# Attention halves of sixteen steps: last scores, value products in groups of four and output copies run in the next half

## The reference, cut

```python
x = x + attn(layernorm(x))                   # 16 heads of 8, 128 tokens against themselves
x = x + cross_attn(layernorm(x), ctx, mask)  # 16 heads of 8, 128 tokens against 77
x = x + moe(layernorm(x))                    # gate on L2-normed projection, top 2 of 8 experts

def attention(q_in, kv_in):                  # the same shape for both
    q, k, v = heads(q_in @ Wq.T), heads(kv_in @ Wk.T), heads(kv_in @ Wv.T)
    scores = einsum("bhqd,bhkd->bhqk", q, k) * scale      # cross: where mask == 0, -1e9
    return einsum("bhqk,bhkd->bhqd", softmax(scores), v) @ Wo.T + bias

def moe(x):                                  # h [8, 64, 128, 512]
    comb = sum(one_hot(top_i, 8) * softmax(top_v)[..., None], -2)
    h = gelu(einsum("bsd,edf->ebsf", x, W1) + b1)
    return einsum("ebsd,bse->bsd", einsum("ebsf,efd->ebsd", h, W2) + b2, comb)
```

## Time and profile before

| what | value |
|---|---|
| three runs | 1179.84, 1180.71, 1183.54 us |
| median | 1180.71 us |
| the profiled execution | 1185.62 us, its span 1183.9 us |
| TensorE busy over the span | 996.1 us, 84% |
| ScalarE | 799.0 us, 67% |
| VectorE | 749.3 us, 63% |
| GpSimd | 593.3 us, 50% |
| mean granted TensorE clock | 0.941 of full speed |
| DMA | 144.16 MB, mean 122 GB/s |

### The profile page before, as it was taken

One profiled execution on the slowest core, in us unless ns is written; L12 is line 12 of the kernel. 1 busy time (PEld: TensorE's weight loads), 2 busy tenths in 40 slices (PEclk: granted clock), 3 DMA queues, 4 the chain that ended last, 5 costly groups with the idle time before them and its releaser, 6 DMA issues. The chain is left out here.

```text
span 1183.9 us, 31785 instructions
## 1 busy us (share of the span) xinstructions
PE 996.1 (84%) x11621; PEld 767.5 (65%) x11621; DVE 749.3 (63%) x2074; ACT 799.0 (67%) x1649; POOL 593.3 (50%) x821
## 2 busy tenths in 40 slices
PE   2567889999999999999999999847529999999940
PEld 1345667777777777777777777635418888888830
DVE  2554746666667666676666674423258888888836
ACT  2144557777777777777777777635419999999930
POOL 4313423365655664664654643544534666666650
PEclk9997999999999999999999999978759999999975
DMA  3337684455455555545545642230452444232319
GB/s 92 83 75 157 141 187 102 120 142 146 128 151 134 134 136 140 142 126 140 151 112 147 147 110 73 57 81 31 136 161 76 125 129 113 79 83 75 84 56 372
DMA packets 120387, 144.16 MB, mean 122 GB/s; under 512 B 34189, under 2 KB 98528, under 8 KB 115432
## 3 DMA queue, kind: packets, MB, share of 16 engines
q1 hardware_dynamic: 108888, 120.33, 40.0%
q0 software_dynamic: 9168, 17.21, 4.8%
q10 hardware_dynamic: 2176, 4.59, 1.0%
HBM read 88.38 MB, written 55.36 MB: 121 GB/s over the span
## 5 line engine op out<-in xcount | busy, mean ns | idle before, releaser
L615 ACT ACTIVATE probs<-sc_a 77x512 f32<-77x512 f32 (+1 forms) x512 | 301.0, 592 | 148.5 <-PE sc_a L1008 93.2
L757 DVE TENSOR_REDUCE negm_m<-sc_m 128x4 f32<-128x512 f32 x256 | 169.5, 683 | 82.5 <-PE sc_m L987 81.4
L1305 POOL DMA_INDIRECT y_d<-yo,row x156 | 160.7, 1030 | 115.0 <-DVE yo L1419 73.6
L757 DVE TENSOR_REDUCE negm_cm<-sc_m 128x4 f32<-128x308 f32 x256 | 119.1, 471 | 144.5 <-PE sc_m L992 143.0
L477 POOL DMA_INDIRECT xs_d<-xrow,slot_i x128 | 131.9, 1031 | 121.3 <-PE sc_a L1008 80.0
L1022 PE MATMUL pv<-probs,big 128*32 128x128 f32 x4096 | 165.7, 280 | 0.6
L987 PE MATMUL sc_m<-ks,qs 96*128 96x128 bf16 x1024 | 105.3, 230 | 37.5 <-DMA ks<-stk_k 13.4
L1022 PEld LDWEIGHTS pv<-probs,big 128*32 128x32 f32 x4096 | 96.3, 109 | 56.2 <-ACT probs L615 28.6
L1400 DVE TENSOR_TENSOR gl<-g,gh 128x512 fp32r<-128x512 f32 x156 | 107.4, 689 | 35.1 <-ACT g L1349 34.6
L987 PEld LDWEIGHTS sc_m<-ks,qs 96*128 96x128 bf16 x1024 | 71.6, 102 | 82.6 <-issue 55.8
L1003 PE MATMUL sc_a<-cqs,cks 102*77 102x128 bf16 x1024 | 102.0, 223 | 4.9 <-DMA cqs<-cmscr 4.8
(11 more groups left out here) (202 smaller groups left out, 2333.7 us busy)
## 6 DMA issues: line engine op xcount, KB each, us to landing
xg<-xs_d SPq DMA_DIRECT2D x39, 260.0 KB
stk_q<-parts_q SPq DMA_DIRECT2D x16, 384.0 KB, 2.9
stk_k<-parts_k SPq DMA_DIRECT2D x16, 384.0 KB, 2.7
qs<-stk_q SPq DMA_DIRECT2D x16, 384.0 KB, 5.9
ks<-stk_k SPq DMA_DIRECT2D x32, 192.0 KB
stk_cq<-parts_cq SPq DMA_DIRECT2D x16, 384.0 KB, 2.9
cqs<-stk_cq SPq DMA_DIRECT2D x16, 384.0 KB
xin<-x_dram SPq DMA_DIRECT2D x16, 256.0 KB
```

Source lines behind the costliest of these rows:

```text
L615: nc.scalar.activation(probs[e % 4][0:rows], sc_a[e % 2][0:rows], ACT.Exp, scale=scale)\
L757: nc.vector.tensor_reduce(out=negm[n][:, s, HG * g + 4 * half:HG * g + 4 * half + 4], in_=sc_m[u % 2][:, 0:4 * cols].rearrange("p (j k) -> ...
L1305: nc.gpsimd.indirect_dma_start(out=y12_d, in_=yo[par][:, c, :], in_offset=None, bounds_check=2 * B * S - 1, oob_is_err=False, out_offset=b ...
```

## The change

A half has 16 steps (`STEPS = UNITS`). What stood in steps 16 to 18 of a half runs inside the first steps of the next: the last unit's `shifted` in step 0, the last four units of `values` in step 2 and the second output copy on ScalarE in step 3. `values` runs in groups of four units, in steps 2, 6, 10 and 14, where before it ran in groups of two. There are seven `probs` tiles (`NP`) in place of four, used in rotation across halves (`probs_of`). The waits for whole halves between two halves are gone: each unit waits for the unit two before it, across the boundary too, and the waits for a half's stacks and folded maxima stand in step 1 (`own_ready`, `cross_ready`).

The tables of side work are written anew on all engines. The output transposes are in steps 2 and 5 of X and 2 and 4 of Y (before: 0 and 1), each output's product in step 9 of X and 8 of Y (before: 5). The transposes of the normalised rows for the cross queries, the cross query product and its splitting into parts move from the end of Y into steps 1 to 6 of the following X, with `dump` and `stack` of "cq". In Y `mark` goes from step 13 to 15, and `weigh` and `route` go into the next X. On SyncE's queue the fold of "m" stands ahead of the stack of "k". GpSimd's body has its pieces in another order to match. No product, exponential, maximum or DMA is added or left out.

The diff, cut to its core:

```diff
-STEPS = UNITS + LEAD + 2
+STEPS = UNITS
...
+NP = 7
...
+        def probs_of(n, b, u):
+
+            half = 2 * b if n == "s" else 2 * b + 5
+            return probs[(UNITS * half + u) % NP]
...
-                        for n, dst in (("cq", cqs), ("ck", cks)):
-                            wait_block(sp, st_f["c"], t - 3)
-                            stack(n, t - 1, dst[1 - par])
+                        wait_block(sp, st_f["c"], t - 3)
+                        stack("ck", t - 1, cks[1 - par])
+                        dump("cq", t - 1)
+                        stack("cq", t - 1, cqs[1 - par])
...
                         fold("m", t + 1, qs[1 - par])
...
+                    if on_(t + 2):
+                        stack("k", t + 2, ks[par])
...
+                    if on_(t - 1):
+                        third("cq", t - 1)
...
+                def exponential(attn, e, before):
...
+                    n, b, rows, scale = attn
+                    act.wait_ge(st_f[n].sem, st_f[n].val(b, e + 1))
+                    if e >= NP:
+                        act.wait_ge(pv_ok[n].sem, pv_ok[n].val(b, e - NP + 1))
+                    elif before:
+                        act.wait_ge(pv_ok[before[0]].sem, pv_ok[before[0]].val(before[1], UNITS - NP + e + 1))
...
+                        if u == 0 and before:
+                            exponential(before, UNITS - 1, None)
+                        if u > 0 and attn:
+                            exponential(attn, u - 1, before)
+                        if u == 3 and before:
+                            out_T(before[0], before[1], 1)
+                        if u == 12 and attn:
+                            out_T(attn[0], attn[1], 0)
                         between(u)
-                    if on_(b):
-                        out_T(n, b, 1)
...
+                        if u == 2 and on_(t - 1):
+                            evac(xnT["2"][:], "x2T", t - 1, 1)
+                        if u == 4 and on_(t - 1):
+                            first("cq", t - 1, bq_c)
+                        if u == 6 and on_(t - 1):
+                            second("cq", t - 1)
...
+                        if u == 8 and on_(t - 3):
+                            evac(onT["c"][:], "onT_c", t - 3, 1)
...
+                        if u == 12 and on_(t):
                             evac(cT[:], "cT", t, 1, TC)
...
+                        if u == 7 and on_(t):
                             evac(onT["s"][:], "onT_s", t, 1)
...
+                        if 12 <= u < 12 + NS and on_(t):
+                            normalise("2", t, x2, u - 12)
+                        if u == 15 and on_(t - 3):
                             act.wait_ge(dv_ok.sem, dv_ok.val(t - 3))
                             nc.scalar.activation(ev[:], dv[:], ACT.Exp).then_inc(ev_ok.sem, 1)
...
+                        if u == 0 and on_(t - 4):
+                            weigh(t - 4)
+                        if u == 1 and on_(t - 4):
+                            route(t - 4)
+                        if u == 3 and on_(t - 3):
+                            divide("c", t - 3, 0)
+                        if u == 4 and on_(t - 1):
+                            wait_block(dve, part3["q"], t + 1)
+                            remainder("cq", t - 1, bq_c)
                         if u == 6 and on_(t - 3):
+                            divide("c", t - 3, 1)
+                        if u == 10 and on_(t - 3):
                             wait_block(dve, x3_st, t - 4)
                             add_residual("c", t - 3, x2res[1 - par], x3)
-                        if u == 7 and on_(t - 3):
...
-                        if u == 12 and on_(t):
+                        if u == 15 and on_(t):
                             wait_block(dve, part3["ck"], t - 1)
                             remainder("ck", t, bk_c)
...
+                        if u == 3 and on_(t):
+                            divide("s", t, 0)
+                        if u == 5 and on_(t):
+                            divide("s", t, 1)
...
                             choose(t - 3)
-                        if u == 13 and on_(t - 3):
+                        if u == 14 and on_(t - 3):
+                            point(t - 3)
+                        if u == 15 and on_(t - 3):
                             mark(t - 3)
...
-                        if u == 18 and on_(t):
-                            wait_block(dve, part3["q"], t + 2)
-                            remainder("cq", t, bq_c)
...
                         pe.wait_ge(max_ok[n].sem, max_ok[n].val(b, u - 1))
+                    else:
+                        wait_block(pe, max_ok[last[0]], last[1], UNITS - 1 + u)
...
+                    else:
+                        wait_block(pe, exp_ok[last[0]], last[1], UNITS - 1 + u)
...
 
                     for u in range(STEPS):
-                        if maxi and u < UNITS:
+                        if maxi:
                             scores(maxi[0], maxi[1], u, *maxi[2:])
-                        if attn:
-                            n, b, qst, kst, va, cols, bias, last = attn
-                            if LEAD <= u < UNITS + LEAD:
-                                shifted(n, b, u - LEAD, qst, kst, cols, bias)
-                            if u >= LEAD + 2 and u % 2 == 0:
-                                values(n, b, u - LEAD - 3, va, last)
-                                values(n, b, u - LEAD - 2, va, last)
+                        if u == 0 and before:
+                            shifted(before[0], before[1], UNITS - 1, *before[2:])
+                        if u == 1 and attn:
+                            ready()
+                        if u > 0 and attn:
+                            shifted(attn[0], attn[1], u - 1, *attn[2:])
+                        if u == 2 and before:
+                            for v in range(UNITS - 4, UNITS):
+                                values(before[0], before[1], v, *before[2:])
+                        if u >= 6 and u % 4 == 2 and attn:
+                            for v in range(u - 6, u - 2):
+                                values(attn[0], attn[1], v, *attn[2:])
                         between(u)
...
                     def in_x(u):
-                        if u < NO and on_(t - 3):
-                            outputs_T("c", t - 3, u)
-                        if u == 3 and on_(t - 3):
+                        if u == 1 and on_(t - 1):
+                            pe.wait_ge(ln_ok["2"].sem, ln_ok["2"].val(t - 1))
+                            transposes("x2T", t - 1, 1, [xn["2"][:, s, :] for s in range(NS)], 128)
+                        if u == 2 and on_(t - 3):
+                            outputs_T("c", t - 3, 0)
+                        if u == 3 and on_(t - 1):
+                            pe.wait_ge(drained["x2T"].sem, drained["x2T"].val(t - 1))
+                            product("cq", t - 1, cw_q[:], xnT["2"][:], T)
+                        if u == 5 and on_(t - 3):
+                            outputs_T("c", t - 3, 1)
+                        if u == 5 and on_(t - 1):
+                            by_token("cv", t - 1, 0, cT, cw_v[:], D, SC)
+                        if u == 7 and on_(t - 3):
                             divided_T("c", t - 3)
-                        if u == 4 and on_(t - 1):
...
                             project("c", t - 3, cw_o)
-                        if u == 6 and on_(t - 2):
-                            maxima_T("cm", t - 2)
...
-                        if u == 11 and on_(t):
+                        if u == 13 and on_(t):
                             pe.wait_ge(drained["cT"].sem, drained["cT"].val(t))
...
-                        if u < NO and on_(t):
-                            outputs_T("s", t, u)
-                        if u == 3 and on_(t):
+                        if u == 2 and on_(t):
+                            outputs_T("s", t, 0)
+                        if u == 4 and on_(t):
+                            outputs_T("s", t, 1)
+                        if u == 4 and on_(t + 1):
...
+                        if u == 8 and on_(t):
                             project("s", t, w_ff)
...
-                        if u == 16 and on_(t):
-                            pe.wait_ge(drained["x2T"].sem, drained["x2T"].val(t))
-                            product("cq", t, cw_q[:], xnT["2"][:], T)
...
+                    beside(own(t), cross(t - 3), maxi, own_ready, in_x)
...
+                    beside(cross(t - 2), own(t), maxi, cross_ready, in_y)
```

219 lines of the change are left out of this document (93 added, 126 removed).

## The result

The changed kernel took 1235.95 us (median of four, 1233.89 to 1237.25) beside 1182.12 for the kernel before; the ratio is 1.0455, interval 1.043 to 1.0481. Run again unedited as a control, on a chip on which the kernel before took 1191.89 us, it took 1240.98: 1.0401 (1.037 to 1.0432). The forecast was slower, 1206, with a range to 1230. The direction held, the size did not: the cost is about twice the forecast, and above the range. The control came out a little under the first ratio; the two intervals meet at their edges.

The account below looks back on a forecast made before the run. TensorE's own queue was taken as the bound. Per iteration 5.3 - 1.6 - 2.1 = +1.6 us, +19 over twelve, +6 for filling and draining: 1185.62 + 25 = 1210.6, less 4.9 for the median, 1206 us; range 1188 to 1230.

Parts of the forecast that it names:

- Grouping: Value groups in X and Y: seven fewer groups, 0.23 us each to enter and leave, save 1.6 us an iteration.
- The alternative of 3.1: If both tiling mode changes around a group cost 0.22, seven groups fewer save 3.1 us an iteration; forecast falls to 1188.
- A to F: Six new TensorE waits on hand-offs after bare steps, three in Y and three in X: 5.3 us an iteration.
- Old waits: Existing TensorE waits, on maxima, last exponentials and smaller ones, go: 2.1 us an iteration; without new waits X 20.0, Y 21.3.
- C: Y, step 15: the rank products wait for `chosen`, whose chain stands behind that step's maximum: 0.9 us.
- The DMA chain: Cross queries and fold through DRAM: landed 22.4 to 24 us into X, wanted at Y's step 1 at 23.9; covered.
- DMA bound: Rival: every landing 2 us later, TensorE waits at Y's step 1 in each iteration, +24, 1230 us; chance 0.10.
- The clock rival: The idle time of every D takes TensorE's clock to the lower level: +20 more, 1226 us; chance 0.14.
- D: X, step 5: second cross transposes wait for bank 1 until VectorE takes the query remainder: 1.9 us, the largest wait.
- Filling and draining: Both ends of the first phase: the cross queries' chain starts later, +6 us together, bounds 0 and 10.
- faster: Rival: waits are not additive, one wait lets the next hand-offs come in time; 1176 us; chance 0.13.
- no change: Rival: switches cost more than read, or two of the forecast waits vanish; 1181 us; chance 0.08.

Follow-up runs that it names:

- all_fixes: The change plus the edits of no_d, handoffs and fold_split, cross keys' stack ahead of two loads, second part of cross queries a step earlier: ratio 0.9721.
- all_twos: all_fixes with value products in groups of two units in every second step instead of four in every fourth: ratio 0.9953.
- no_d: The change with first part and remainder of cross queries one step earlier, and step 5's value product ahead of the second output transposes: ratio 1.0244.
- handoffs: The change with four ScalarE copies one step earlier and the rank products moved to step 1 of the next X: ratio 1.0260.
- cross_fold: The change with the dump of the folded cross maxima issued ahead of the cross queries' stack on SyncE, its read behind it: ratio 1.0318.
- fold_split: The change with both fold dumps, cross and own, issued ahead of the query or key stack on SyncE, their reads behind it: ratio 1.0218.

## Why the prediction was wrong, step by step

- **What bounds the kernel.** Right. Every change of an iteration in these runs is TensorE's own place or a wait of it.
- **Grouping, 1.6 an iteration.** Undersized: 1.9 by the pair of all_fixes and all_twos. The alternative of 3.1, and with it 1188, came from a double count (0.44 a group, see all_twos). Taken alone in the kernel before it brought nothing, because the groups had been cover; the sum had that cover in the waits A to F and so was not wrong by it.
- **Old waits, 2.1; halves without waits of 20.0 and 21.3.** The halves are right: 20.07 and 21.22 by the trace of the change. With 1.9 for the grouping the old waits come to about 1.8, within their bounds; no run took them away alone.
- **A to F, 5.3 an iteration.** The places and five of the six sizes are right; C is 1.17 instead of 0.9, since the chain to `chosen` also waits behind the index search of step 14. Together 5.75 against 5.3, 0.4 an iteration, 5 us. no_d and handoffs show that they are real and additive.
- **The DMA chain, "covered, with little to spare".** This step failed. Its term for the fold's dump was 3.4 us, read where the first phase drains; in the steady part of the changed kernel it is 5.6 on average and up to 6.9. Even the steady part of the kernel before had 4.6, which would have left the chain only 0.3 ahead of its user (22.4 + 1.2 against 23.9). TensorE's wait there was 0.5 an iteration on average, 6 us, and cross_fold took it away. The rival that had it (DMA bound) was right in kind and far too large at 2 us an iteration.
- **The clock rival.** Partly: "every D" did not take the clock down, two of eleven did, 3 us. The forecast had it at nothing or 20.
- **Filling and draining, 6 with bounds 0 and 10.** This is the other failed step, and the largest error: 8.2 at the start and, of the 12.3 at the end, about 11 beyond what one more ordinary iteration would explain at 1.6. The sum had let only the cross queries' later start count. At the start it was the keys' stack behind the fold: the prediction had it land 2 us before X, as it does in the steady part, and fold_split recovers 8 to 11 us. At the end TensorE's waits for DMAs went down, from 21 to 15 us, and those for other engines up, from 7 to 22: the hand-offs went on there, and the sum had none of them beyond the twelfth iteration. The runs show how both hang together. That stretch, 165.8 and 168.5 in the two traces of the change and 152.8 before, is still 165.0 in handoffs, where longer DMA waits (21 us) take their place, 161.4 in fold_split and 162.0 in cross_fold, and only with all fixes 151.2.
- **The rivals faster and no change.** Their argument, that waits at one place let the next hand-off come in time, is refuted by six waits of the forecast size in each iteration.

Added up for the spans, eleven iterations and the two ends: 25 forecast; +5 for the hand-offs (mostly C), +6 for the fold, +3 for the clock, +13 for the two ends, together 52, measured 51.6.
